# Reordering VectorE, GpSimd and DMA work in the two transformer layers of an adaLN block (one core)

## The reference, cut to what matters

```python
def _layer(x, wqkv, qs, ksc, wo, lg, lb, w1, b1, w2, b2):
    h = shift_token(x)                       # second half of the columns, one token later
    q, k, v = split(h @ wqkv)
    q = l2norm(q) * qs; k = l2norm(k) * ksc  # per head
    q, k = rotary_xpos(q, k)
    o = local_attention(q, k, v)             # own window and the one before
    x = x + o @ wo
    h = shift_token(x)
    h = (h - mu) / sqrt(var + 1e-05) * lg + lb
    a, g = split(h @ w1 + b1)
    return x + (a * gelu(g)) @ w2 + b2
```

## Time and profile before

| | |
|---|---|
| median of 3 runs | 2208.16 us (2204.4 to 2209.06) |
| profiled execution | 2207.61 us, span 2205.8 us |
| busy, share of the span | PE 85%, DVE 68%, ACT 54%, POOL 45% |
| chain that ended last | PE 35%, DVE 18%, issue 6%, ACT 5%, rest below 3% |

### The profile page before, as it was taken

The page is one execution under the profiler, slowest core; times in us unless marked ns, Lnnn a source line. Parts: engine busy times, 40 slices in busy tenths (PEclk is TensorE's granted clock), DMA queues, the critical chain, the costliest instruction groups (busy, mean ns, idle before and its releaser), DMA issues.

```text
span 2205.8 us, 36469 instructions
## 1 busy us (share of the span) xinstructions
PE 1865.4 (85%) x12941; PEld 1403.2 (64%) x12941; DVE 1510.0 (68%) x3723; ACT 1186.2 (54%) x2717; POOL 996.6 (45%) x788
## 2 busy tenths in 40 slices
PE   5569999999954799888899888987888999888986
PEld 3444444444433587776777867766776777777776
DVE  3678878877653685766867758584776857768673
ACT  0545545443433656656566565664656566565562
POOL 0325544647463444444444435543545445454451
PEclk7779999999976999999999999998999999999998
DMA  4000010101024000000000002011000000000000
GB/s 141 24 26 27 1 34 11 41 16 51 15 67 134 11 20 17 19 12 24 20 17 21 10 26 68 17 53 32 25 16 29 27 26 25 18 30 26 26 18 22
DMA packets 83407, 68.58 MB, mean 31 GB/s; under 512 B 10853, under 2 KB 79509, under 8 KB 83225
## 3 DMA queue, kind: packets, MB, share of 16 engines
q1 hardware_dynamic: 83224, 66.25, 9.7%
HBM read 45.22 MB, written 16.81 MB: 28 GB/s over the span
## 4 chain that ended last, share of the span: by engine, by line
PE 35%; DVE 18%; issue 6%; ACT 5%; DMA 2%; SPq 1%; POOL 1%; DVEq 0%; ACTq 0%; POOLq 0%
PE bank_O L1201 4%; PE bank_T L1189 3%; PE bank_A L260 3%; PE bank_A L262 3%; PE bank_P L260 3%; PE bank_A L261 3%; ACT l_sm L1337 3%; PE bank_P L261 2%; PE bank_P L262 2%; DVE l_t L1512 2%; PE bank_A L1178 2%; DVE l_sm L1528 2%; DVE l_u_lo L1594 2%; PE bank_T L1168 2%; PE bank_T L260 1%
## 5 line engine op out<-in xcount | busy, mean ns | idle before, releaser
L1737 POOL TENSOR_TENSOR l_sm<-l_sm,l_rinv 128x512 f32<-128x512 f32 (+1 forms) x256 | 250.1, 998 | 366.1 <-DVE l_rinv L1536 365.8
L1725 POOL TENSOR_TENSOR l_t<-l_qk,l_tab 128x512 f32<-128x512 f32 x128 | 170.1, 1350 | 328.8 <-DVE l_ss L1495 328.8
L1337 ACT ACTIVATE l_sm<-l_sm,l_nb 128x256 f32<-128x256 f32 (+1 forms) x512 | 248.1, 486 | 82.0 <-DVE l_nb L1528 81.8
L260 PE MATMUL bank_A<-l_f_hi,l_w_hi 128*114 128x256 f32 (+1 forms) x768 | 220.1, 287 | 3.7 <-DVE l_f_lo L1573 2.7
L262 PE MATMUL bank_A<-l_f_hi,l_w_lo 128*114 128x256 f32 (+1 forms) x768 | 216.0, 281 | 0.0
L261 PE MATMUL bank_A<-l_f_lo,l_w_hi 128*114 128x256 f32 (+1 forms) x768 | 215.8, 281 | 0.0
L1528 DVE CUSTOM_DVE_ANT_0 l_sm<-bank_A,l_mask 128x256 f32<-128x256 f32 (+1 forms) x512 | 177.1, 401 | 52.0 <-PE bank_A L1178 51.5
L1189 PE MATMUL bank_T<-ident,l_sm 128*128 128x128 f32 x960 | 149.1, 290 | 65.7 <-POOL l_sm L1737 34.4
L618 ACT ACTIVATE pr<-ps_S 128x1024 f32<-128x1024 f32 x128 | 130.7, 1023 | 125.4 <-PE ps_S L512 124.6
L1594 DVE TENSOR_TENSOR l_u_lo<-l_up,l_u_hi 114x256 fp32r<-114x256 f32 (+1 forms) x192 | 197.8, 1036 | 0.1
L861 POOL TENSOR_TENSOR acc<-acc,pr 128x1024 f32<-128x1024 f32 x64 | 155.8, 2435 | 51.0 <-ACT pr L618 46.5
(11 more groups left out here) (268 smaller groups left out, 5127.3 us busy)
## 6 DMA issues: line engine op xcount, KB each, us to landing
l_xs<-x_layers SPq DMA_DIRECT2D x64, 128.0 KB, 2.5
x<-in_x SPq DMA_DIRECT2D x8, 512.0 KB, 3.9
base_rows<-x SPq DMA_DIRECT2D x16, 256.0 KB, 2.1
x_layers<-x SPq DMA_DIRECT2D x16, 256.0 KB, 2.1
l_xs<-x_layers SPq DMA_DIRECT2D x64, 64.0 KB, 2.2
x_layers<-l_yb SPq DMA_DIRECT2D x32, 128.0 KB, 1.8
l_base<-base_rows SPq DMA_DIRECT2D x32, 128.0 KB, 3.1
out<-l_yb SPq DMA_DIRECT2D x32, 128.0 KB, 1.7
```

The source lines that it names most:

```text
L260: pe.matmul(out, a_hi, b_hi, start=(start and k == 0), stop=False)
L1337: eng.activation(row, row, ACT.Exp, bias=nb[:, R % SS, e:e + 1], scale=-1.0, accum_out=rsum[:, R % SS, e:e + 1]).then_inc(ex_ready, 1)
L1725: eng.tensor_tensor(dst[:, :, :, lo:lo + H2], src[:, :, :, hi:hi + H2], table[:, :, 1, lo:lo + H2].unsqueeze(2).to_broadcast([P, 2, LH, H2 ...
L1737: eng.tensor_tensor(row, row, rinv[:, R % SS, :].unsqueeze(2).to_broadcast([P, 2, P * windows(n)]), ALU.mult).then_inc(pn_ready, 1)
```

## The change

Nothing is computed otherwise. The calls move:

- **DVE.** `norms` of following +2 and +3 goes from round 1 to slot 14 of the turn before. `rotated` is cut in `added` and `rotated`, in rounds 3 and 4 for +2 and 6 and 7 for +3 (before: 3 and 5). `o_split` of +1 to +3 stands ahead of the slot's `inverse`. `h_split` of following +1 goes from slot 1 to slot 0, `deviation` from slot 1 to 2. `residual` of +3: slot 6 to 5; `moments` of +2: 5 to 6; `moments` of +3, `norms` of following +0 and +1, and `layer_norm` of +2 and +3: slot 8 to 7, which is now ahead of the `h_split` that opens slot 8; `rotated` of following +0 and +1 from slots 9, 10 to 8, 9. The last `u_split` and `y_out` of a group go behind the first minima of the next.
- **PE, ACT.** `h_transpose`/`h_out` of following +1: slot 1 to 0. `project` of +3: slot 6 to 5. `qk_transpose`/`qk_out` of +2 and +3: rounds 4, 6 to 6, 8.
- **POOL.** `finish` of the first two units of a group: from its end to round 2 of the next. `tables(1)` in four parts, rounds 8 to 11.
- **Weight pieces.** Those of wqkv one a round (5 to 8, 10, 11); those of wo and w1 in rounds 4, 5, 9, 10; those of w2 are loaded behind the shifted copies of +2 and +3 and split in slots 7, 9 and 11, through `pt` and one old buffer. The small scale rows of layer 2 load in group 1.

```diff
-        W_Q = {2: (0, 1), 3: (2, 3), 8: (4, 5)}
-        W_O = {2: (0, 1)}
-        W_1 = {3: (0, 1), 7: (2, 3), 8: (4, 5)}
+        W_Q = {5: (0,), 6: (1,), 7: (2,), 8: (3,), 10: (4,), 11: (5,)}
+        W_O = {4: (0, 1)}
+        W_1 = {5: (0, 1), 9: (2, 3), 10: (4, 5)}
...
 PE
-                        if r in (4, 6):
-                            qk_transpose(first + 2 + (r - 4) // 2)
+                        if r in (6, 8):
+                            qk_transpose(first + 2 + (r - 6) // 2)
...
-                        if k in (0, 4, 6):
-                            project(first + (1, 0, 2, 3)[k // 2])
+                        if k in (0, 4, 5):
+                            project(first + max(1, k - 2))
...
+                        if k == 0 and ahead:
+                            h_transpose(following + 1)
...
 ACT
-                        if g == GL and k == 0:
-                            piece_2(0), piece_2(1), piece_2(2)
+                        if g == GL and k in (7, 9, 11):
+                            piece_2((k - 7) // 2)
...
 DVE
-                        if r == 4 and g >= 1:
-                            y_out(2 * g - 1)
...
-                        if r == 1:
-                            norms(first // 2 + 1)
-                        if r in (3, 5):
-                            rotated(first + 2 + (r - 3) // 2)
+                        if r == 0 and g >= 1:
+                            u_split(m0 - 1)
+                        if r == 1 and g >= 1:
+                            y_out(2 * g - 2)
+                        if r in (3, 6):
+                            added(first + 1 + r // 3)
+                        if r in (4, 7):
+                            rotated(first + 1 + r // 3)
+                        if r == 5 and g >= 1:
+                            y_out(2 * g - 1)
...
+                        if k in (0, 2, 4):
+                            o_split(first + 1 + k // 2)
                         if k < 3:
                             inverse(*head(first, r - 2)), inverse(*head(first, r - 1))
-                        if k in (0, 2, 4):
-                            o_split(first + 1 + k // 2)
...
                         if k == 0:
                             residual(first + 1)
+                            if ahead:
+                                h_split(following + 1)
                             moments(first)
                         if k == 1:
-                            if ahead:
-                                h_split(following + 1)
                             moments(first + 1)
+                        if k == 2:
                             deviation(first // 2)
-                        if k == 2:
                             layer_norm(first // 2, rs)
...
                         if k == 5:
+                            residual(first + 3)
+                        if k == 6:
                             moments(first + 2)
-                        if k == 6:
-                            residual(first + 3)
-                        if k == 8:
+                        if k == 7:
                             moments(first + 3)
...
-                    if k == 8 and ahead:
+                    if k == 7 and ahead:
                         norms(following // 2, also=first // 2 + 1 if g >= 0 else None)
...
-                    if k in (9, 10) and ahead:
-                        rotated(following + k - 9)
+                    if k in (8, 9) and ahead:
+                        added(following + k - 8)
+                        rotated(following + k - 8)
+                    if k == 14 and ahead:
+                        norms(following // 2 + 1)
...
                     up_out(m0 + HC - 1)
-                    u_split(m0 + HC - 2), u_split(m0 + HC - 1)
-                    y_out(2 * g)
+                    u_split(m0 + HC - 2)
...
 POOL
-                        if r == 6 and g >= 1:
-                            finish(first - 2), finish(first - 1)
+                        if r in (2, 6) and g >= 1:
+                            finish(first - 4 + r // 3), finish(first - 3 + r // 3)
...
+                        if g == GL - 1 and r in (8, 9, 10, 11):
+                            tables(1, r - 8)
...
 SP
+                if g == GL:
+                    take_2(0)
                 shift(first + 3)
+                if g == GL:
+                    take_2(1), take_2(2)
```

More of the change, by code:

```diff
@@ L1507, in norms, with added @@
                 rsqrt(eng, link, rn[:, q % 2, 0:n], ss[:, q % 2, 0:n], ra[:, 0:n])
-            def rotated(n):
+            def added(n):
                 w.wait_ge(trig_ready, 3 * n + 3)
@@ L1512, in rotated @@
                 eng.tensor_tensor(a, a, t2[:, n % 2], ALU.add).then_inc(t2_used, 1)
+            def rotated(n):
+                a = t1[:, n % 2]
                 w.wait_ge(t2_used, n + 1)
@@ L1583, in up_out @@
                     w.wait_ge(w1_ready, KC + 6)
-                    w.wait_ge(w2_ready, 2 + 3)
                 if m >= 3:
@@ L1626, in _ @@
                 if g == GROUPS:
-                    y_out(2 * g - 1)
+                    u_split(m0 - 1)
+                    y_out(2 * g - 2), y_out(2 * g - 1)
                     break
@@ L1782, in piece_2 @@
                                   w2[0][0:n, 2 * i:2 * i + 2, :].rearrange("p c n -> p (c n)").bitcast(F32), ALU.subtract).then_inc(w2_ready, 1)
-            tables(0)
+            for i in range(4):
+                tables(0, i)
             for g in range(-1, GROUPS + 1):
@@ L1788, in _ @@
                 if g == GROUPS:
-                    finish(first - 2), finish(first - 1)
+                    for n in range(first - QUAD, first):
+                        finish(n)
                     break
@@ L1818, in _ @@
                         first_w2_wo()
-                if g >= 0:
-                    finish(first), finish(first + 1)
         @block.sync
@@ L1878, in store, with table, scale @@
                 eng.dma_start(dst, yb[:, n % QUAD, :]).then_inc(y_stored[n % QUAD], 16)
-            def tables(l):
+            def table(l):
                 eng.dma_start(tab[:, :, :, :].rearrange("p t c d -> p t (c d)"), io["rope"].rearrange("t p c d -> p t (c d)")).then_inc(tab_loaded, 16)
+            def scale(l):
                 for i, name in enumerate(("q_scale", "k_scale")):
@@ L1886, in tables, with take @@
                     eng.dma_start(scales[:, 2 * i + 1, HD // 2:HD], row[:, 0:HD // 2].to_broadcast([P, HD // 2])).then_inc(tab_loaded, 16)
-            def take(dst, src):
-                eng.dma_start(dst, src).then_inc(piece_loaded, 16)
+            def take(dst, src, loaded=piece_loaded):
+                eng.dma_start(dst, src).then_inc(loaded, 16)
             def take_q():
@@ L1914, in take_rest, with take_2 @@
                     take_1(i)
+            def take_2(i):
                 w.wait_ge(w1_ready, KC + 6)
-                for i in range(3):
-                    n = CS[2 * i]
-                    take(AT_2[i][0:n, :].rearrange("p (c n) -> p c n", c=2),
-                         io["w2"][1, CO[2 * i]:CO[2 * i] + 2 * n, :].rearrange("(c p) n -> p c n", c=2))
+                w.wait_ge(pv_done, PAIRS * QUAD * (GL + 1))
+                n = CS[2 * i]
+                take(AT_2[i][0:n, :].rearrange("p (c n) -> p c n", c=2),
+                     io["w2"][1, CO[2 * i]:CO[2 * i] + 2 * n, :].rearrange("(c p) n -> p c n", c=2), w2_loaded if i else piece_loaded)
             load(0), load(1)
@@ L1923, in _ @@
             load(2), load(3)
-            tables(0)
+            table(0), scale(0)
             w2_v = io["w2"]
@@ L1946, in _ @@
                     w.wait_ge(trig_ready, 3 * UL)
-                    tables(1)
+                    table(1)
                 if g == GL:
                     take_rest()
+                if g == 1:
+                    w.wait_ge(tab_ready, 4)
+                    scale(1)
                 if g >= 1:
```

34 lines of the change are left out of this document (17 added, 17 removed).

## The result

The changed kernel takes 2275.3 us (median of 4 runs, 2274.25 to 2277.22), the kernel before 2208.6 on the same chip: ratio 1.0306, 95% interval 1.0288 to 1.0324, so 67 us or 3.1% slower. The forecast was 2230: right in sign, inside the range, but a third of the size.

The account below looks back on a forecast made before the run. PE was taken as the bound, working almost without a break, with gaps mostly from late DVE. +2.2 us in 15 groups (+33) and -10.5 once gave +22.5 on 2207.6: 2230 us, range 2165 to 2280.

Parts of the forecast that it names:

- Slots 0 to 3, -1.8: Slots 0 to 3: gaps of 1.48 and 1.74 us go, 1.4 comes back; -1.8 us a period.
- Slots 5 to 9, +1.4: Slot 9: `norms` held by `trig` delays `h_split`; a 3.0 us stall replaces 0.95 and 0.66; +1.4 us a period.
- Slots 13 to 15, +2.3: Slot 14: `norms` beside `trig` delays `up_out`; first scores wait 3.0 us, a 0.96 wait goes; +2.3 us a period.
- rival "faster": First scores wait for nothing in slot 14, -1.1 us a period: 2181 us, or 2140 with slot 9 unblocked; chance 0.33.
- Rounds 3 to 8, +0.3: Later `rotated` removes 0.87 us; a longer wait than 0.97 returns at `project` of +0; +0.3 us a period.
- The period: Sum of the four slot and round terms: +2.2 us a group, +33 us for 15 groups.
- The step that failed: PE's clock after the two 3.0 us stalls: taken to stay up, since 3.0 is below the 3.59 followed by half clock.
- The case was among the rivals, at 0.18: The clock falls too, behind one stall each group: 14 x 3.3 = +46 us, 2276 us; chance 0.18.
- Group 7, -3: Group 7: one weight piece a round frees ACT for `pt_out`; 3 us back once.
- Group 8: Group 8: w2 loads behind the shifted copies remove an 11.52 us wait; 7 us taken back once.
- the last group: Last group: waits of 4.15 and 6.01 us for `o_split` and `layer_norm` shorten; -3.5 us once.
- `finish` was set at nothing: Layer 2: four more POOL operations before the next probabilities, set against those removed at the group's start; no net cost.

Follow-up runs that it names:

- e6: The kernel before with only the change's slots 0 to 3 part (`h_transpose`, `h_out`, `h_split`, `o_split`, `deviation` moved): 2186.38 us, ratio 0.9904.
- e8: The changed kernel with `trig` of unit +3 moved behind the next group's first probabilities, so POOL is idle beside slot 14's `norms`: 2274.56 us, one run.
- e9: The changed kernel with PE transposing a constant before its two stalls (20 times before slot 9's `qkv`, 18 before the first scores): 2246.72 us, ratio 1.0166.
- e11: The kernel of e10 with group 7's wqkv pieces and rotary tables back in their old places: 2187.45 us, ratio 0.9906.
- e5: The kernel of e3 with `added` and `rotated` of following +0 and +1 back in slots 9 and 10: 2208.74 us, ratio 1.0006.
- e10: The kernel of e5 with `finish` calls moved from rounds 2 and 6 to rounds 6 and 8: 2192.97 us, ratio 0.9934.
- e4: The changed kernel with two Newton steps in `norms` instead of three: 2237.44 us, ratio 1.0134.
- e1: The changed kernel with `norms` of units +2 and +3 back in round 1 instead of slot 14: 2229.65 us, ratio 1.0096.
- e3: The changed kernel with `norms` of +2, +3 back in round 1 and `h_split` of following +3 ahead of `norms` in slot 7: 2222.16 us, ratio 1.0067.

## Why the prediction was right in sign and wrong in size

**Slots 0 to 3, -1.8.** Right in the main: `e6` alone gives -1.5 a period in layer 1, -1.3 in layer 2. The 128x2 forms of `deviation` are blocked as assumed (0.98 and 0.96 us). By the rule of the Trainium skill (SBUF — State Buffer, "Who interferes with whom"), as the prediction used it, they are blocked whatever their size; the trace agrees on the size with these two numbers. But the two held operations have one SBUF input each, so the rule for two inputs does not cover them. The same section of the Trainium skill counts `tensor_scalar`, which they are, among the operations that can block and be blocked through a two-port mode; no run here shows which mode they ran in.

**Slots 5 to 9, +1.4.** The step by step sum from the end of `sums` to the end of `h_split` was 8.9 us and measured 1182.44 - 1173.50 = 8.9; the stall is 3.09 for 3.0.

**Slots 13 to 15, +2.3.** The stall is 3.06 for 3.0, for the reason given. The rival "faster" asked for a `norms` that is not blocked; `e8` frees it by moving `trig` and gains nothing, as POOL's work lands on the probabilities instead. A `norms` freed without that price was not run.

**Rounds 3 to 8, +0.3.** The waits of 0.87 and 0.97 became 0.39, 0.30 and 1.21, the last in front of `project` as foreseen: +0.1. With the shorter waits of these rounds, which the forecast left out (0.30 and 0.56 before, 0.47 and 0.16 after, in group 4), it is -0.2.

**The period.** Their sum, +2.2, is more than a period costs when the clock does not fall: 1.3 in the seven groups of `e9` at 1.00. The 2.2 of all 12 agree with the forecast by luck, since falls of the clock are in them. The waits were foreseen in place and length, and the forecast of their sum was 0.9 too high, of which rounds 3 to 8 make 0.5.

**The step that failed** is the one that kept the clock out of the forecast: "Gaps up to 1.74 in group 4 left 1.00. My two stalls of 3.0 lie between" and "3.0 is below 3.59". Two gaps of 3.0 to 3.1 us a group bring TensorE to its lower level for 3 us or more, behind 23 of the 24 such gaps in ordinary groups; `e9` takes most of this away with the stalls in place and gives 29 us back, where the forecast fell short by 45. The case was among the rivals, at 0.18, and priced at 3.3 us a group; measured it is some 3.0 in the 12 ordinary ones (4.3 less 1.3), 36 us, and some 6 in group 0 (99.4 us after, 93.2 in `e9`). So its price was about right. That its 2276 is the measured time is in part chance: the waits cost 10 us less than forecast in the ordinary groups, and the next term 10 more.

**Group 7, -3,** had the wrong sign: +9.2 in place of -0.8, and +9.0 in `e9`. "One piece a round frees ACT" did not count that a quarter of the tables waits for its load ahead of probabilities. `e11`, which puts tables and pieces back, gives 6 us of it back. **Group 8** (-4.8, measured -3.5) and **the last group** (-3.5, -3.7) were right. `finish` was set at nothing; in the changed kernel it is nothing, because the stalls cover it. Without them it costs some 2 us a period in layer 2 (`e5` against `e10`).

A row of the kernel before had it, in a group that the forecast did not look into: at the start of group 12 PE waits 2.15 us (its timeline), and the two windows behind show the lower level.

```profile
1845.35 0.41 PE L1189 MATMUL bank_T<-ident,l_sm 128*128 128x128 f32 x2 [2.15 <-POOL l_sm L1737]
```
```profile
1846.00:1848.00 2.00, 2.00 (x10) 1.28 (x10) 1.97 (x2) 1.14 (x6) 0.00 (x0) 0.52 0.20 57
1848.00:1850.00 2.00, 2.00 (x14) 1.45 (x12) 2.00 (x11) 0.72 (x3) 1.13 (x2) 0.63 0.00 0
```

So 3.0 was not between a harmless 1.74 and a harmful 3.59, but above a length that had already done harm; the rival deserved more than 0.18. The expectation of `e4`, which took gaps up to 2.15 us for harmless, missed the same row.

Left open: why the same gap of 3.1 us brings the clock down in one group and not in another. Of the 1.7 us that come back in slots 0 to 3 (3.2 removed, 1.5 gained) 1.0 was followed to its calls in `e6`; of the other 0.7 it is only known that 0.6 is busy time of PE.

## What to carry to other kernels

Where the same order of work repeats, price a new idle time of TensorE twice: its length, and the stretch of half clock that may follow; here a stall of 3.1 us cost 3.1 + 2.3 where the clock fell. If such a stall can't be avoided, work on constants in it is worth more than nothing. A chain of small DVE operations has the length of the POOL work beside it, so place it where POOL is idle, and then ask what POOL's displaced work holds up. And split a change by stage before judging it: one part of this one, with the weight pieces, makes the kernel 1.2% faster, while the whole is 3.1% slower.

## What the runs showed of the hardware that was not expected

- The length of a gap alone does not say whether the clock falls: 3.09 us left it at 1.00 in group 3 of `e1`, 3.10 brought 0.50 in group 4. The 2.15 us above did it too, and in `e3` 0.97 and 1.89 us with some 3 us of work between them, in three of the six ordinary groups of layer 1 (90.7 us instead of 89.1).
- Two one-input operations of 128x2 are held for 0.98 and 0.96 us beside two POOL operations of 1.0 us; from the second POOL operation's end all small operations of `deviation` take 0.16 us.
- The block works both ways: beside DVE's `added` and `rotated` the products of `trig` took 3.50 and 3.33 us in round 2 of `e8`, and 2.52 and 2.58 in slot 12, with neither beside them.
